# A gated attention and expert layer: VectorE's order inside the attention groups, and four expert tiles written out on TensorE

## The reference, cut to what matters

```python
x = x + tanh(g_xattn[0]) * xattn(ctx_768, layernorm(x), mask, ...)     # x: (4, 1024, 256), ctx: (4, 64, 192)
x = x + tanh(g_ffn[0])   * ffn(layernorm(x), w_router, w1, b1, w2, b2)

# xattn: q from the latents (x), k and v from the context and the latents, 4 heads of 64
q = ln @ Wq.T;  kv = concatenate([xn @ Wkv.T, ln @ Wlkv.T], axis=1)
qn = rmsnorm(q, qn_g) * SCALE;  kn = rmsnorm(k, kn_g)
out = softmax(where(mask, qn @ kn.T, -max)) @ v;   return out @ Wo.T + bo

# ffn: 8 experts, each token goes to its best 2
logits = xf @ w_router;  probs = softmax(logits);  topk_w, topk_idx = top_k(probs, 2)
h = gelu(einsum('te,ieh->tih', xf, w1) + b1);   out = einsum('tih,ihe->tie', h, w2) + b2
return sum(out * weights[..., None], axis=1)
```

## Time and profile before

| what | value |
|---|---|
| median of 3 runs | 905.99 us (902.59 to 906.76) |
| the profiled execution | 906.47 us, its span 904.7 us |
| TensorE matmul (PE) busy | 855.7 us, 95% of the span |
| VectorE (DVE) | 645.3 us, 71% |
| ScalarE (ACT) | 511.5 us, 57% |
| GpSimd (POOL) | 289.5 us, 32% |
| TensorE clock granted | 0.987 of full speed over the span |

### The profile page before, as it was taken

How to read it: one execution, slowest core, us unless ns; L and a number is a source line. 1 busy time by engine, 2 the same in 40 slices (tenths; PEclk the granted TensorE clock), 3 DMA queues, 4 the chain that set the end, 5 groups by cost and what they waited for, 6 DMA issues and landing times.

```text
span 904.7 us, 19559 instructions
## 1 busy us (share of the span) xinstructions
PE 855.7 (95%) x5968; PEld 657.3 (73%) x5968; DVE 645.3 (71%) x1500; ACT 511.5 (57%) x1371; POOL 289.5 (32%) x241
## 2 busy tenths in 40 slices
PE   3898999999999999999999999899999999999995
PEld 3654555545555455555469999899999999999995
DVE  6766777768777667676897777775755776676695
ACT  2668875787857877468841843443433443353462
POOL 2321212221265212641054238332332322232233
PEclk8899999999999999999999999999999999999998
DMA  4801000130012201120044649352442535362272
GB/s 128 248 1 50 1 1 1 47 96 1 7 54 82 94 1 56 50 94 1 2 137 99 181 82 259 58 144 47 96 90 43 137 72 114 47 145 45 37 230 27
DMA packets 71896, 70.26 MB, mean 78 GB/s; under 512 B 18593, under 2 KB 66977, under 8 KB 71841
## 3 DMA queue, kind: packets, MB, share of 16 engines
q1 hardware_dynamic: 57696, 52.73, 20.0%
q0 software_dynamic: 13152, 16.86, 10.9%
q10 hardware_dynamic: 992, 0.00, 0.1%
HBM read 44.04 MB, written 26.31 MB: 78 GB/s over the span
## 4 chain that ended last, share of the span: by engine, by line
PE 56%; DVE 17%; issue 13%; POOL 8%; ACT 4%; DMA 1%; another core or an unknown queue 0%; SPq 0%; POOLq 0%; DVEq 0%; ACTq 0%
PE psS L1705 22%; PE psF L1901 10%; PE psO L1901 10%; DVE p_sum L1141 6%; PE psS L1822 4%; POOL rr L681 4%; POOL routed L691 3%; PE psO L1838 3%; PE psF L1705 2%; PE psF L1869 1%; ACT sq L828 1%; DMA xr<-in_x 1%; PE psO L1850 1%; DVE Q L1124 1%; PE psO L1705 1%
## 5 line engine op out<-in xcount | busy, mean ns | idle before, releaser
L889 ACT ACTIVATE V<-psS,b_col 128x256 f32<-128x256 f32 x280 | 116.9, 470 | 214.8 <-PE psS L1705 195.3
L699 POOL DMA_INDIRECT out<-V,token_i x70 | 121.5, 1736 | 261.8 <-DVE V L1332 240.5
L872 ACT ACTIVATE p_ring<-psS,shift 128x1024 f32<-128x1024 f32 x128 | 136.6, 1111 | 71.7 <-PE psS L1822 69.7
L681 POOL TENSOR_TENSOR rr<-ssm,minus_half 128x4 f32<-128x4 f32 (+1 forms) x72 | 76.1, 1057 | 282.4 <-DVE ssm L1105 282.4
L1838 PE MATMUL psO<-p_ring,V 128*64 128x512 f32 x576 | 148.5, 612 | 0.0
L1141 DVE TENSOR_TENSOR p_sum<-p_sum,p_ring 128x1024 f32<-128x1024 f32 (+1 forms) x112 | 135.7, 1211 | 1.3
L1901 PE MATMUL psF<-ln_hi,K 128*128 128x256 f32 x560 | 124.2, 285 | 0.2
L1822 PEld LDWEIGHTS psS<-Q,K 64*128 64x128 f32 x864 | 77.0, 187 | 61.3 <-issue 41.9
L1822 PE MATMUL psS<-Q,K 64*128 64x512 f32 x864 | 121.3, 413 | 0.0
L1901 PE MATMUL psO<-ln_hi,K 128*128 128x256 f32 x560 | 120.5, 279 | 0.0
L1309 DVE CAST K<-V 128x512 fp32r<-128x512 f32 x140 | 60.4, 431 | 59.1 <-ACT V L889 57.0
(11 more groups left out here) (297 smaller groups left out, 1766.5 us busy)
## 6 DMA issues: line engine op xcount, KB each, us to landing
xr<-in_L_ffn_w SPq DMA_DIRECT2D x11, 1024.0 KB, 8.2
xn<-in_L_ffn_w SPq DMA_DIRECT2D x11, 1024.0 KB, 5.6
lnf<-routed SPq DMA_DIRECT2D x35, 258.0 KB
routed<-pad_rows SPq DMA_DIRECT2D x17, 258.0 KB, 9.9
xr<-in_x SPq DMA_DIRECT2D x8, 512.0 KB, 4.5
xb<-in_x SPq DMA_DIRECT2D x4, 1024.0 KB, 6.1
out<-xb SPq DMA_DIRECT2D x4, 1024.0 KB
b_raw<-in_L_ffn_b SPq DMA_DIRECT2D x11, 128.0 KB, 3.5
```

Of the source, the lines that this page charges most:

```text
L681: pool.tensor_tensor(rr[0:p, c % 2, n], ssm[0:p, c % 2, n], minus_half[0:p, n], ALU.pow).then_inc(rr_ready, 1)
L699: pool.indirect_dma_start(out_rows, bass.IndirectOffsetOnAxis(ap=token_i[:, m:m + 1], axis=0), y_out[:, m, :], None, bounds_check=NTOK - 1 ...
L872: act.activation(p_ring[0:p, u % RING, :], psS[u % 2][0:p].rearrange("p a n -> p (a n)"), ACT.Exp, bias=bias).then_inc(exp_done, 1)
L889: act.activation(g32[:, q % 2, (c % 2) * TM:(c % 2 + 1) * TM], psH[q][:, (c % 2) * TM:(c % 2 + 1) * TM], ACT.Gelu_apprx_tanh, bias=b1_col[ ...
```

## The change

VectorE's first addition of a group moves behind `heads_lo` and `mean_squares`, in groups that project a tile, except those with i = 0 or 5, group 0, and the two groups in which router logits are taken at i = 3. These are 48 of the 72 groups. The offsets of batch 1 are made at the end of group 4 and not of group 5. In tile 7, `plan_experts` moves from before `move_meta` and `turned_lo(8)` to behind them, next to `plan_switches`. On TensorE tiles 5 to 8 are written out with the same calls, and the loop covers tiles 9 to 15.

```diff
@@ VectorE, attention group g @@
+                    summed = summed_at(g) is not None
+                    routed_here = not even and past and not last and i == 3
+                    between = tile_at(g) is not None and g >= 1 and i != 0 and i != 5 and not routed_here
-                    if g >= 1:
+                    if g >= 1 and not between:
                         add_probabilities(2 * g - 2)
...
                     if tile_at(g) is not None:
                         mean_squares(tile_at(g))
-                    if not even and past and not last and i == 3:
+                    if between:
+                        add_probabilities(2 * g - 2)
+                    if routed_here:
                         router_logits(b - 1)
-                    summed = summed_at(g) is not None
                     if g >= 1 and not ahead and summed:
                         add_probabilities(2 * g - 1)
...
-                    if even and more and b == 0 and i == 5:
+                    if even and more and b == 0 and i == 4:
                         norm_offsets(b + 1)
@@ VectorE, tiles 5 to 8 @@
                 for t in range(5, KTILES):
                     for q in range(NQ):
                         activate(t, q)
-                    if t == 7:
-                        plan_experts()
                     move_meta(t)
                     turned_lo(t + 1)
                     take_meta(t + 1)
...
                         if t == 7:
+                            plan_experts()
                             plan_switches()
                         results(t)
@@ TensorE @@
-                with pe.Fori(5, SURE - 1) as t:
+                for t in range(5, KTILES):
+                    first_layer(t)
+                    turn_tile(t + 1)
+                    second_layer(t)
+
+                with pe.Fori(KTILES, SURE - 1) as t:
                     first_layer(t)
                     turn_tile(t + 1)
                     second_layer(t)
```

## The result

| what | before | after |
|---|---|---|
| median on the same chip | 904.56 us (6 runs, 902.59 to 906.76) | 909.87 us (6 runs, 907.46 to 912.32) |
| ratio after / before | | 1.0061, interval 1.0043 to 1.0079 |
| the profiled execution's span | 904.7 us | 908.9 us |
| start of the first tile's first layer | 462.56 us | 470.75 us |
| last tile's first layer | 883.72 us | 887.89 us |

The change costs 0.6%, where I had forecast 896.5 us and a range of 890 to 902. The two marks at the foot of the table divide it: the attention stage is 8.2 us longer (470.75 - 462.56) and the expert stage 4.0 us shorter (417.14 against 421.16 between the two marks). From the start of group 3's scores to the end of the last group's scores it is 7.7 us more than before.

The account below looks back on a forecast made before the run. TensorE bounds the attention stage, with 18.35 us of gaps. Attention gain 5.93 + 1.42 + 1.2 - 0.3 = 8.25, say 8.2 us; 906.47 - 8.2 - 1.5 = 896.8, forecast 896.5 us, range 890 to 902.

Parts of the forecast that it names:

- What bounds it: Attention stage, 40 to 470 us: TensorE is busy 411.65 of 430 us, leaving 18.35 us to win.
- The nine waits: Attention: nine TensorE waits for qkd, with the addition ahead of ssm, close when it moves; 5.93 us won.
- What the new order costs: VectorE, attention: addition slightly outlasts the root's 1.12 us idle, qkd up to 0.15 us late; 0.3 us lost, bounds 0 to 3.2.
- The groups with i = 5: Attention: the 3.0 us of TensorE waits for probability sums lie in these groups; nothing won.
- Offsets: Attention: offsets made at the end of group 4 remove ScalarE's 1.92 us idle and TensorE's wait; 1.42 us won.
- Bank waits: Attention, L1764, groups with i = 7: heads_lo comes some 0.4 us sooner in three waits; 1.2 us won.
- Tile 7: Expert stage: turned_lo(8) comes 1.7 us sooner, tile 9's row load just in time; 1.5 us won, bounds 0.5 and 1.6.
- Written-out tiles: TensorE tiles 5 to 8: four more code packets on q8 cost 0, bounds 0 and 10 us.
- A: Expert stage: tile 7's stall belongs to TensorE's loop and goes away, tile 9's rows then bind; 891.5 us, chance 0.20.
- B: Only part arrives: half the attention gaps, or 21 groups pay 0.15 us each, or tile 7's stall grows; 901 us, chance 0.19.
- C: Expert stage: late code packets on q8 stall TensorE in the written-out tiles; about 926 us, chance 0.06.
- D: Attention: the ring of probability tiles makes ScalarE wait where TensorE waited, change does nothing; 906 us, chance 0.05.

Follow-up runs that it names:

- e14: Before with offsets and plan moved, first addition moved in nine late groups (one-input, left out of denominators) and groups 25, 43, 61: 905.57 us, attention -6.9 us.
- e15: Before with offsets and plan moved, and the addition between heads_lo and mean_squares in groups 25, 43 and 61 alone: 902.94 us, 0.9977.
- e10: Before with offsets and plan moved, first addition (two inputs) moved in nine late groups and in groups 25, 43, 61: 898.97 us, 0.9993.
- e2: Before with the new place of VectorE's first addition alone: 912.51 us, 1.0100, attention +9.2 us.
- e13: The change with moved additions as one-input reductions, except those opening a sum (left out of denominators): 906.82 us, 1.0026, 36 tiles instead of 35; attention -6.3 us.
- e5: Before with only the offsets of batch 1 moved to the end of group 4: 897.95 us, 0.9979.
- e6: Before with only plan_experts moved behind turned_lo(8) in tile 7: 900.30 us, 1.0003.
- e3: Before with only tiles 5 to 8 written out on TensorE: 903.99 us, 0.9994.
- e12: The changed kernel run again on the third chip, against before there: 907.84 us, 1.0087.
- e4: The change with the first addition behind scale_heads, where no root runs beside it: 930.49 us, 1.0292.
- e11: The change with the moved addition cut in two, half before and half behind scale_heads: 919.99 us, 1.0219.
- e1: The change with the first addition back in its old place in all groups: 900.09 us, 0.9958.

## Why the prediction was wrong, by its own steps

**What bounds it** was right: TensorE, with 18.35 us of gaps, and the gaps stood where I read them.

**The nine waits, 5.93 us.** The step was right in its chain and wrong in its premise. Taken alone without the lock the nine moves give 6.3 us (e14 less e15). With it they give 0.3 us (e10 less e15). The premise that failed is "GpSimd works (1.12 us idle)": the time is the root's own only while no two-input operation of VectorE's has started ahead of it.

**What the new order costs, 0.3 us, bounds 0 to 3.2.** This is the term that failed. I set the addition's 1.23 us against the idle 1.12 us and got 0.15 us per group, taking the two to run side by side. They don't: addition, then 0.87 us more. `qkd` comes 2.18 us after `ssm`, not 1.28, some 0.9 us in 39 of 40 groups. Where the addition had been ahead of `ssm` and had delayed it, the move should still pay about 0.3 us (1.21 - 0.9, an estimate; six waits of e10 are 0.22 to 0.25 us shorter). Where VectorE had waited for the squares anyway (21 groups, 13.6 us), the addition had been free and now costs the whole 0.9 us, less what `qkd` was early by. Even 21 x 0.9 = 19 us was possible, six times my upper bound. What arrived is 9.2 us (e2), or 14 us against the same order with one input (after against e13). I had the long roots of before in reach, at 90.65 and in five more groups.

**The groups with i = 5, nothing.** Wrong: their waits for sums rose from 3.0 to 8.2 us (after, e2) and fell back to 3.0 in e13. Five of the six waits grew by 0.90 to 0.93 us each, and a seventh of 0.63 us came in. The path of the first of them is in the timelines, of before and then of after:

```profile
172.59 0.42 DVE L1115 TENSOR_TENSOR qkd<-psF,rr 128x256 f32<-128x256 f32 x1 [1.12 <-POOL rr L681]
...
176.88 1.08 PE L1850 MATMUL psO<-p_sum,ones 128*64 128x512 f32 x4 [0.16 <-DVE p_sum L1141]
```
```profile
175.23 0.42 DVE L1115 TENSOR_TENSOR qkd<-psF,rr 128x256 f32<-128x256 f32 x1 [0.90 <-POOL rr L681]
...
179.52 1.08 PE L1853 MATMUL psO<-p_sum,ones 128*64 128x512 f32 x4 [1.08 <-DVE p_sum L1141]
```

From `qkd` of the group with i = 4 to TensorE's use of the sum it is 4.29 us in both: VectorE works without a pause from the one to the last addition of the sum, so the 0.9 us of the long root comes out there whole.

**Offsets, 1.42 us.** Right: -1.6 us alone (e5). In after the normed rows start at 68.90 with no wait.

**Bank waits, 1.2 us.** The rows of L1764 are gone in after, but the gain was not seen. In e15, which has the addition ahead of `mean_squares` (in the change it stands behind), the three groups win 0.36 us each and the next group loses 0.75, together 1.0 us lost (-0.6 against -1.6). In after the same three groups have a new wait for `qkd`, 0.38 to 0.40 us each, ahead of the turn, and in e13 as well: both have a long root in the group before. What the change's own placement is worth without any lock was not run.

**Tile 7, 1.5 us.** `plan_experts` moved as told and TensorE's wait for `w_lo` went, but the plan alone gives nothing (e6, 1.0003). The step "just in time" for the row load of tile 9 was too kind: it comes 1.38 us late in after and 0.37 in e6. The 4.0 us that the expert stage gained in after belong to another thing. On the first and the fourth chip TensorE issues slowly for some us near tiles 7 and 8: each of the nine profiles taken there has 1 to 6 gaps of over 0.25 us without a wait on record between the turns of tiles 5 and 10. None of the eight profiles of the other two chips has one, and there turn 5 to turn 10 takes 61.4 to 64.5 us in every kernel. The slow stretch falls differently from kernel to kernel: 67.4 in before, 66.5 in e3, 64.3 in e2, 63.1 in after. On a chip without it the change is slower by 0.87% (e12), more than the 0.61% on the first. What makes TensorE slow there stays open.

**Written-out tiles, 0.** Right (e3, 0.9994). q8 has 30 packets in after, four more than in the earlier trace rows, as counted, and they cost nothing. Their times were read a little wrong: the last one of before starts at 545.3 us, and of the four more of e3 three come between 561 and 599 us and one at 680.

**The rivals.** A: the loop was not the cause of the slow stretch (e3), though its second half, the load of tile 9 behind the last scatter, is what binds now. (Its terms add up to 576.5 us, not 576.9, which would have made it 0.4 us faster.) B: its "the 21 groups pay their 0.15 us each" named the right groups with a sixth of the price. C: did not happen; I looked for the slower side in the code fetch and gave it 0.06. D: in e4 and e11 that mechanism costs 20 to 28 us, in the change 2.4 us. None of the four was the case: the lock was not among them. The chance of 0.06 for slower was the result of listing mechanisms without asking what two engines share when an edit makes them run at the same time.

**What to ship.** Moving the offsets alone is 0.2% faster than before (e5). e1 (offsets, plan, written-out tiles, old order) had 0.9958 on the first chip, in part from the slow stretch of tile 7 (turn 5 to turn 10 in 65.1 us).

## What to carry to other kernels

Filling an engine's idle time with an operation is free only if that operation does not hold up the one that is waited for: before putting a VectorE operation with two SBUF inputs beside a GpSimd operation, find in the trace a place where the two already overlap, and read there how long the GpSimd one takes and which of the two had started first. Look at the spread of an operation's durations (min, median, max) and not only at one instance: a few long ones among many equal ones name what the edit is about to make common. And an operation that hands back a ring slot can be moved only as far as the ring is long.

## What was not expected of the hardware

A root on 128x4 elements, 1.01 us alone, takes 1.92 us beside a two-input addition of 1.21 us that began 0.16 us earlier: it ends 0.87 us after the addition does. Beside a half addition the median is 1.39 us, and beside a reduction of 1.21 us with one input 1.01 us. With an addition that begins 0.20 us after the root it is 1.01 us as well, and the addition takes its usual 1.23 us. The clock granted was 1.00 from 40 to 470 us in before and in after, so none of it is TensorE's clock.
